# The carry of a chunked selective scan added in PSUM: two identity matmuls per tile on TensorE, where VectorE did an add

## The reference

```python
A = -jnp.exp(A_log)
deltaBC = jnp.einsum('bld,od->blo', x, W_bc)          # dt_r, B, C
delta = jax.nn.softplus(dt + b_dt)
def step(h, inp):
    delta_t, B_t, C_t, u_t = inp
    dA = jnp.exp(delta_t[:, :, None] * A[None])
    dBu = (delta_t * u_t)[:, :, None] * B_t[:, None, :]
    h = dA * h + dBu
    y_t = jnp.einsum('bdn,bn->bd', h, C_t)
    return (h, y_t)
```

## Time and profile before

| | |
|---|---|
| median of 3 runs | 1120.57 us (1117.51 to 1124.8) |
| the profiled execution: time | 1123.69 us |
| its span | 1122.0 us |
| scan stage | 224.4 to 853.3 us, 628.9 us, 256 steps |
| PE busy in the span | 911.9 us (81%) |
| DVE busy in the span | 964.6 us (86%) |
| ACT, POOL busy | 460.1 us (41%), 392.1 us (35%) |
| mean granted TensorE clock | 0.869 of 2.4 GHz |

### The profile page before, as it was taken

The page is one execution under the profiler, slowest core; times in us unless marked ns, Lnnn a source line. Parts: engine busy times, 40 slices in busy tenths (PEclk is TensorE's granted clock), DMA queues, the critical chain, the costliest instruction groups (busy, mean ns, idle before and its releaser), DMA issues. The chain is left out here.

```text
span 1122.0 us, 22454 instructions
## 1 busy us (share of the span) xinstructions
PE 911.9 (81%) x7152; PEld 562.7 (50%) x7152; DVE 964.6 (86%) x1164; ACT 460.1 (41%) x887; POOL 392.1 (35%) x690
## 2 busy tenths in 40 slices
PE   5654673489999999999999999999997856666662
PEld 4343442356656656556566566565553444343442
DVE  6664664099999999999999999999998599999993
ACT  2545544434444444444444444444431333333320
POOL 6435432233333333333333333333343244444321
PEclk9675555589999999999999999999998977787786
DMA  9399995931211112121111211111142001111001
GB/s 319 64 147 205 162 135 131 134 108 50 64 52 59 54 52 64 51 62 53 59 55 50 66 51 61 55 55 57 52 139 70 16 0 57 56 56 56 19 19 37
DMA packets 206068, 85.68 MB, mean 76 GB/s; under 512 B 139220, under 2 KB 196052, under 8 KB 205268
## 3 DMA queue, kind: packets, MB, share of 16 engines
q1 hardware_dynamic: 206036, 85.30, 31.9%
HBM read 45.85 MB, written 39.42 MB: 76 GB/s over the span
## 5 line engine op out<-in xcount | busy, mean ns | idle before, releaser
L1439 DVE TENSOR_TENSOR_SCAN arena<-arena,psum 128x1024 f32<-128x1024 f32 x256 | 585.4, 2287 | 8.9
L1260 ACT ACTIVATE arena<-psum 128x512 f32<-128x512 f32 x512 | 281.9, 605 | 347.5 <-PE psum L1123 346.1
L1167 PEld LDWEIGHTS psum<-du_mov,b_sta 96*128 96x128 bf16 x2048 | 199.7, 130 | 237.2 <-issue 217.3
L1136 PE MATMUL psum<-arena,c_sta 128*32 128x256 f32 x2048 | 284.0, 636 | 2.7 <-DVE arena L1439 2.7
L1167 PE MATMUL psum<-du_mov,b_sta 96*128 96x128 bf16 x2048 | 271.2, 313 | 15.2 <-DVE arena L1439 15.2
L1018 POOL TENSOR_TENSOR carry<-arena 128x64 f32<-128x64 f32 x252 | 117.0, 464 | 399.2 <-DVE arena L1439 390.5
L1123 PE MATMUL psum<-delta_mov,a_sta 96*128 96x128 bf16 x2048 | 171.6, 228 | 8.3 <-ACT arena L1260 8.3
L1123 PEld LDWEIGHTS psum<-delta_mov,a_sta 96*128 96x128 bf16 x2048 | 151.9, 110 | 11.3 <-ACT arena L1260 10.2
L1021 POOL TENSOR_TENSOR arena<-zeros 128x64 f32<-128x64 f32 x256 | 78.1, 305 | 20.1
L1436 DVE TENSOR_TENSOR psum<-psum,carry 128x64 f32<-128x64 f32 x256 | 55.3, 216 | 31.3 <-DMA delta_terms<-arena 30.8
L433 PE MATMUL psum<-delta_mov,arena 128*128 128x512 f32 x128 | 75.7, 677 | 0.0
(11 more groups left out here) (142 smaller groups left out, 962.8 us busy)
## 6 DMA issues: line engine op xcount, KB each, us to landing
du_terms<-arena SPq DMA_DIRECT2D x48, 256.0 KB, 3.8
du_mov<-du_terms SPq DMA_DIRECT2D x128, 96.0 KB
b_terms<-delta_mov SPq DMA_DIRECT2D x6, 1024.0 KB, 11.3
delta_terms<-arena SPq DMA_DIRECT2D x48, 128.0 KB, 5.3
delta_mov<-delta_terms SPq DMA_DIRECT2D x128, 48.0 KB
b_sta<-b_terms SPq DMA_DIRECT2D x64, 96.0 KB
arena<-in_L_attn_x SPq DMA_DIRECT2D x8, 512.0 KB, 5.5
base<-arena SPq DMA_DIRECT2D x8, 512.0 KB, 4.7
```

The lines of the kernel that those rows point to most:

```text
L1136: mm = nc.tensor.matmul(psum[32 * j:32 * j + 32, (6 + k) * BANK:(6 + k) * BANK + D], c_sta[k][:, t * 32:(t + 1) * 32], sub(arena, 0, P, (2 ...
L1167: mm = nc.tensor.matmul(sub(psum, 0, P, o, (4, 4), (TS, GD // 2)), b_sta[k][0:ROWS, (s * 4 + tg) * P:(s * 4 + tg + 1) * P], sub(du_mov[k], ...
L1260: nc.scalar.activation(sub(arena, 0, P, k * CHUNK_ELEMS + u * 16 * TS, (TS, 16), (D * TS, SUBS), (1, TS)), sub(psum, 0, P, (4 + u % 2) * B ...
L1439: nc.vector.tensor_tensor_scan(state[s][:, seg], decay[k][:, (s * D + g * GD) * TS:(s * D + (g + 1) * GD) * TS], psum[:, 2 * (step % 2) * ...
```

## The change

Three things are done. DVE no longer adds the carry, and the semaphore carried is gone. PE adds it: after the B group it waits for carry_ready of the same step and issues two f32 matmuls, one per bank, with the 128x128 identity as the stationary operand and 32 elements of the carry as the moving one; they accumulate (start=False) onto the first time steps, and b_ready now comes from the second of them. The eight matmuls of the B group are reordered: before, the two banks took turns; now all four of one bank come first, in the order tg = 1, 2, 3, 0, then four of the other. POOL, which may not overwrite a carry that is still to be read, waits for b_ready where it waited for carried.

```diff
                             if not early:
+                                pool.wait_ge(S["b_ready"], G - 3)
                                 pool.wait_ge(S["scan_done"], G - 3)
-                                pool.wait_ge(S["carried"], G - 3)
...
-                            for tg in range(TS // 4):
-                                for half in range(2):
+                            for half in range(2):
+                                for tg in (1, 2, 3, 0):
...
                                         start=True, stop=True)
+                            pe.wait_ge(S["carry_ready"], G + 1)
+                            for half in range(2):
+                                mm = nc.tensor.matmul(
+                                    sub(psum, 0, P, (pair_bank + half) * BANK, (TS, GD // 2)), ident[:, :],
+                                    carry[:, g, half * (GD // 2):(half + 1) * (GD // 2)],
+                                    start=False, stop=True, skip_group_check=True)
                             mm.then_inc(S["b_ready"], 1)
...
-                            firsts = sub(psum, 0, P, 2 * (step % 2) * BANK, (TS, GD))
-                            nc.vector.tensor_tensor(firsts, firsts, carry[:, g, :], ALU.add)\
-                                .then_inc(S["carried"], 1)
-                            dve.wait_ge(S["carried"], G + 1)
                             nc.vector.tensor_tensor_scan(
```

More of the change, by code:

```diff
@@ L119, in bank @@
             return psum[:, i * BANK:(i + n) * BANK]
-        names = """own_made b_filled a_sta_zeroed c_sta_zeroed carried f_seed f_newton f_keep wv_sum wv_mean
+        names = """own_made b_filled a_sta_zeroed c_sta_zeroed f_seed f_newton f_keep wv_sum wv_mean
             wv_centred weights_loaded ident_zeroed ident_ready zeros_ready wT_psum wT_ready a_exp a_neg a_hi
```

## The result

The changed kernel takes 1215.1 us (median; 1214.74 to 1223.37) against 1120.57 before: 1.0855 times as long, 95% interval 1.0816 to 1.0894. The forecast was 1232 with a range of 1212 to 1266: the right side and mechanism, 17 us too high. Ratios and intervals here are of fast executions alone; a single one of this case, 1202.41 us in the kernel without the add, ran in the chip's slower state and is left out.

What follows compares the result with a forecast made beforehand. PE was taken to bound the scan stage; 244 full steps x 0.45 us gave +110 us, with first and last steps +111 us, hence 1232 us against the median, range 1212 to 1266.

Steps and rivals of the forecast that it cites:

- PE sets the pace, by a hair: Scan stage's middle: PE needs about 2.47 us a step, DVE 2.44, so work added to PE lengthens the step.
- Four records at 0.113 us, 0.45 us a step: Two f32 identity matmuls on PE make four records; over 244 full steps they add 110 us.
- halfway to a bf16 row: Range's lower end: identity group at 0.37 us, between 0.45 and 0.29 from the argument group's bf16 records; 1212 us.
- The order of the B group is worth nothing; the step in its output is to blame: B group on PE: reordering banks gains nothing; stepped output explains 0.105 against 0.0725 us a record. Rival, order pays: 8%.
- The wait for the carry and POOL's new wait cost nothing: PE asks for the carry some 7 us after POOL makes it; POOL's b_ready wait is long fulfilled. Rival, PE waits: 3%.
- First and last steps: Ends of the scan stage: first four, two at half clock, +1.8 us less 2 x 0.15; last eight +0 to 0.4.
- Mode switches beside the identity group: Rival: PE switches working mode on both sides of the identity group, 0.73 us a step, 1300 us; chance 10%.
- the 0.14 us that the prediction read in rows 9: B group on PE takes 0.98 us before a contraction, 0.84 before an argument group; read as one mode switch.
- DVE as the pace: Rival: DVE sets the scan stage's pace, so the step falls from 2.466 to 2.31 us, 1081 us; chance 4%.

Runs made afterwards that it cites:

- PE's half of the change alone: Kernel before with the new B order, wait for carry_ready and two identity matmuls on zeros, DVE's add kept: 1214.76 us, ratio 1.0819.
- DVE's half alone: Kernel before without DVE's add and nothing in its place, the carry left out of the computation: ratio 0.9976.
- contraction in twos: Kernel before with the contraction issued for two groups of channels in every second step instead of one in each: 1117.76 us, ratio 0.9972.
- second pair: Changed kernel with two more f32 identity matmuls on zeros behind the first two: 1330.02 us, ratio 1.1856.
- either edit alone: Kernel before with only DVE's add left out, ratio 0.9976, or only the contraction issued for two groups every second step, ratio 0.9972.
- both: Kernel before with the contraction issued for two groups every second step and DVE's add left out, no carry: 1091.75 us, ratio 0.9717.

## Why the prediction was right, point by point

**PE sets the pace, by a hair.** Right, and shown from both sides: PE's half of the change alone gives the whole result (1214.76 us), DVE's half alone nothing that can be told (0.9976, interval to 1.0007). That the margin was a hair is shown by the contraction in twos: a little off PE, and DVE leads at 2.446 us. One thing in it is not explained: taking the add away makes the full steps a little shorter as well (last section).

**Four records at 0.113 us, 0.45 us a step.** This is the term of the sum that was too large. The measured price is 0.37 us: 0.41 to the next group's start, and 0.04 back from the argument group, 0.54 instead of 0.58. The rows were right for records in a row, as the second pair shows (0.45). What the sum left out is the edges: the first identity record follows a B record, and the group behind them no longer does. 244 steps at 0.37 are 90 us instead of 110. On the median of before that gives 1120.6 + 90 + 1.5 = 1212, the lower end of the range; the result lies 3 us above it. That the range held it is luck: its lower end, 0.37 us, was drawn halfway to a bf16 row, and the edges of the group, which are the true reason, stood nowhere in the sum. DVE's share of the stage came out at 81% instead of 78% for the same reason, a step of 2.84 us instead of 2.92.

**The order of the B group is worth nothing; the step in its output is to blame.** Right: 1.0008 and 721.7 against 720.9 us for the order, and 0.45 instead of 0.84 us for eight records without the step.

**The wait for the carry and POOL's new wait cost nothing.** Right for the full steps: among PE's waits of the changed kernel none is on POOL. In two of the first steps the trace puts 2.0 us of the scan's waits down to POOL's L1021, but the scan at 238.90 begins 1.09 us behind the start of its identity group (237.81), just as the scan at 235.65 does behind its own (234.56), where the trace names PE.

**First and last steps.** The first steps were taken as 1.8 us longer, two of them at half clock. In the changed kernel PE had waited 10.6 us for the first scan and then found a granted clock of 0.50 from 232.9 to 243 us, so three steps ran at 1.2 GHz and not two: its B groups of 236.19 and 239.44 us are 3.25 us apart, against 2.53.

```profile
236.19 1.91 PE L1167 MATMUL psum<-du_mov,b_sta 96*128 96x128 bf16 x8
237.81 0.98 PE L1174 MATMUL psum<-carry,ident 128*128 128x32 f32 x4
...
238.60 1.04 PE L1123 MATMUL psum<-delta_mov,a_sta 96*128 96x128 bf16 x8
...
239.44 1.91 PE L1167 MATMUL psum<-du_mov,b_sta 96*128 96x128 bf16 x8
```

The identity group takes 0.79 us there, twice its 0.41. The last steps became shorter, not longer: the last seven intervals between scans take 2.39 us on the mean against 2.45 before, since the 0.98 us from the B group to the contraction was kept in the sum, while in the changed kernel B group and identity group take 0.84 and 0.51 us there (934.08 to the contraction at 934.59) and the contraction 1.04. Both ends together are what is left of 91.9 us beside 90: 2 us, against 1.5 in the sum; that these agree is chance.

**The rivals.** Mode switches beside the identity group: none showed in the full steps, where its neighbours are 128 columns wide. In the last chunk, where the contraction follows it, it takes 0.51 us instead of 0.41, although both are f32; so a price like the 0.14 us that the prediction read in rows 9 is real. It was worth 5.3 us of scan span with DVE's add in place and 24 without. Whether the tiles of 32 columns make it or the 256 moving elements, no run separates. DVE as the pace: refuted. What it would have won was also taken too small: the forecast took 2.31 us for scans back to back, and they take 2.20.

## What to carry to other kernels

When two engines are busy 100% and 98.5% of a stage, moving work from one to the other is a loss by the full price on the receiving side. The shares over the whole span (86% and 81%) can name the wrong one: the order of starts and unused room before each group decide it. Price an operation by the start-to-start distance of its neighbours in the very place where it will stand, edges included, and prefer a type that loads its weights fast: here the addition cost 0.37 us in f32 and 0.10 - 0.04 = 0.06 in bf16, with the carry rounded. A balanced pair of engines gives little back until both are relieved: 6.2 and 5.3 us for either edit alone, 30.3 for both (629.0 - 598.7).

## What the runs showed that was not expected

- A pair of bf16 identity matmuls cost almost nothing: 637.9 - 629.0 = 8.9 us of scan span for 512 matmuls, and the add on DVE gone.
- Without the add, and with PE's list unchanged, the scan span fell by 6.2 us. The first and last steps, which DVE leads, can explain about half. The full steps became shorter as well, 2.454 us on the mean between 400 and 760 us against 2.468, and all of it lies between the start of PE's contraction and the next B group, 1.031 us on the mean against 1.045. Why is open; it was not tried.
- An output stepped by 16 floats nearly doubles the time of a 128-column bf16 matmul (0.105 us against 0.056) but is free beneath an f32 weight load (0.112 us a record with it, 0.113 without).
